# Turning a pair of heads' sums as they lie, and adding the two strips of keys on VectorE

## The reference

```python
qkv = _ln(x, ln1_g, ln1_b) @ w_in.T + b_in
q, k, v = ...                                  # 16 heads of 16
scores = einsum('bhqd,bhkd->bhqk', q, k) / sqrt(16)
allowed = (idx % 8 == 0)[:, None] | (idx[:, None] == idx[None, :])
attn = softmax(where(allowed, scores, -inf))
o = einsum('bhqk,bhkd->bhqd', attn, v)
x = x + o @ w_out.T + b_out
```

## Time and profile before

| | |
|---|---|
| median of 3 runs | 1451.54 us (1450.45 to 1452.65) |
| profiled execution, its own time | 1452.35 us |
| its span | 1450.6 us |
| PE busy | 1404.0 us, 97% |
| DVE busy | 846.5 us, 58% |
| ACT busy | 721.7 us, 50% |
| POOL busy | 649.0 us, 45% |
| mean granted TensorE clock | 0.993 of full speed |

### The profile page before, as it was taken

One profiled execution on the slowest core, in us unless ns is written; L12 is line 12 of the kernel. 1 busy time (PEld: TensorE's weight loads), 2 busy tenths in 40 slices (PEclk: granted clock), 3 DMA queues, 4 the chain that ended last, 5 costly groups with the idle time before them and its releaser, 6 DMA issues.

```text
span 1450.6 us, 26449 instructions
## 1 busy us (share of the span) xinstructions
PE 1404.0 (97%) x10167; PEld 1063.0 (73%) x10167; DVE 846.5 (58%) x1792; ACT 721.7 (50%) x1071; POOL 649.0 (45%) x533
## 2 busy tenths in 40 slices
PE   6889999999999999999999999999999999999997
PEld 4778655678888766668888866666888875557996
DVE  7747676636656666555647575763566556762332
ACT  3444555554444555554444555555344455555442
POOL 4554321338754414145865431333776441132755
PEclk9899999999999999999999999999999999999999
DMA  7464123215561222212682213220556212310100
GB/s 251 158 177 103 50 51 66 55 41 190 186 163 44 58 59 50 55 44 81 205 211 69 76 31 79 55 55 16 166 188 166 87 38 50 79 26 23 52 15 30
DMA packets 91393, 130.50 MB, mean 90 GB/s; under 512 B 8314, under 2 KB 68180, under 8 KB 88148
## 3 DMA queue, kind: packets, MB, share of 16 engines
q1 hardware_dynamic: 91268, 128.82, 32.2%
HBM read 68.08 MB, written 60.57 MB: 89 GB/s over the span
## 4 chain that ended last, share of the span: by engine, by line
PE 78%; DVE 11%; POOL 5%; issue 2%; ACT 1%; DMA 1%; SPq 0%; POOLq 0%; DVEq 0%; ACTq 0%
PE ps L1550 19%; PE ps L1551 16%; PE ps L1552 16%; PE ps L1739 9%; PE ps L1728 6%; PE ps L1713 4%; DVE mx L1428 3%; PE ps L1787 2%; DVE stats L1302 2%; PE ps L1775 2%; PE ps L1809 2%; POOL rows L1034 2%; PE ps L1745 1%; PE ps L1671 1%; DVE xn L1390 1%
## 5 line engine op out<-in xcount | busy, mean ns | idle before, releaser
L1428 DVE TENSOR_REDUCE mx<-ps 128x2 f32<-128x1024 f32 x256 | 311.1, 1223 | 189.9 <-PE ps L1713 188.3
L1157 ACT ACTIVATE prob<-ps 128x1024 f32<-128x1024 f32 x256 | 261.8, 1023 | 139.1 <-PE ps L1728 138.8
L1049 POOL TENSOR_TENSOR hid1l<-gel,hid1h 128x512 fp32r<-128x512 f32 x85 | 111.3, 1310 | 207.1 <-ACT hid1h L1199 206.9
L1049 POOL TENSOR_TENSOR hid2l<-gel,hid2h 128x512 fp32r<-128x512 f32 x85 | 111.4, 1311 | 201.6 <-ACT hid2h L1199 201.6
L1049 POOL TENSOR_TENSOR hid0l<-gel,hid0h 128x512 fp32r<-128x512 f32 x86 | 112.5, 1308 | 194.2 <-ACT hid0h L1199 194.2
L1191 ACT ACTIVATE gel<-ps,cols 128x512 f32<-128x512 f32 x128 | 88.1, 688 | 181.0 <-PE ps L1552 169.9
L1739 PE MATMUL ps<-prob,vals 128*32 128x256 f32 x2048 | 163.6, 391 | 0.0
L1193 ACT ACTIVATE gel<-ps 128x512 f32<-128x512 f32 x128 | 76.5, 598 | 170.6 <-PE ps L1809 170.6
L1728 PE MATMUL ps<-qslot,kslot 50*128 50x256 f32 x1024 | 128.9, 330 | 1.8 <-ACT prob L1157 1.8
L1728 PEld LDWEIGHTS ps<-qslot,kslot 50*128 50x128 f32 x1024 | 76.2, 184 | 66.5 <-issue 46.9
L1713 PE MATMUL ps<-kslot,qslot 48*128 48x512 f32 x512 | 102.3, 410 | 3.5 <-DVE mx L1428 3.0
(11 more groups left out here) (244 smaller groups left out, 3956.5 us busy)
## 6 DMA issues: line engine op xcount, KB each, us to landing
k_d<-kst SPq DMA_DIRECT2D x192, 128.0 KB
kslot<-k_d SPq DMA_DIRECT2D x64, 384.0 KB
xin<-in_L_attn_x SPq DMA_DIRECT2D x32, 256.0 KB, 4.0
rows<-xs_d SPq DMA_DIRECT2D x16, 512.0 KB, 6.0
y_d<-rows SPq DMA_DIRECT2D x15, 512.0 KB, 3.1
rows<-y_d SPq DMA_DIRECT2D x15, 512.0 KB, 4.3
out<-rows SPq DMA_DIRECT2D x15, 512.0 KB, 3.9
xs_d<-xin SPq DMA_DIRECT2D x28, 256.0 KB, 2.7
```

The lines of the kernel that those rows point to most:

```text
L1049: nc.gpsimd.tensor_tensor(hid[i % RING][1][:], gel[i % 2][:], hid[i % RING][0][:], ALU.subtract).then_inc(lo_done, 1)
L1157: nc.scalar.activation(prob[(n - 1) % 2][:].rearrange("p e i q -> p (e i q)"), ps[:, 0:2, :].rearrange("p a n -> p (a n)"), ACT.Exp).then_ ...
L1428: nc.vector.tensor_reduce(best[:, :, j % NQ], ps[:, at:at + 2, :], AX.X, ALU.max).then_inc(maxr_done, 1)
```

## The change

`fold` goes, with the instruction that makes it, and the three counts of the setup go down by one. PE turns each half of `oraw` with the plain identity: one transpose of 128 x 128 in the place of one product of 128 x 64. The result has 128 columns for a half in the place of 64, and the two strips lie beside one another. DVE copies the first strip of both halves to a new tile `osum` in SBUF (68 numbers for a partition), and adds the second strip from PSUM to it. It takes the reciprocal from `osum` and multiplies `osum` by it. The next user of the bank on PE waits for the addition (`osum_done`), and no longer for the multiplications (`otok_done`).

```diff
-COLS, BIN_DONE, CVB = 2, 9, 16
+COLS, BIN_DONE, CVB = 1, 8, 15
...
-                link(nc.vector.tensor_tensor(fold[:], ident[:, 0:2 * PR], ident[:, 2 * PR:4 * PR], ALU.add), False)
...
+        osum = keep("osum", [P, NQ, 2, VW])
...
-                    o = ps[:, BANK[(what, *a)], 0:NQ * 2 * PR].rearrange("p (t e v) -> p t e v", t=NQ, e=2)
-                    nc.vector.reciprocal(rsum[:], o[:, :, :, HD]).then_inc(rsum_done, 1)
+                    o = ps[:, BANK[(what, *a)], 0:NQ * P].rearrange("p (t i e v) -> p t i e v", t=NQ, i=2, e=2)
+
+                    nc.vector.tensor_copy(osum[:], o[:, :, 0, :, 0:VW]).then_inc(osum_done, 1)
+                    dve.wait_ge(osum_done, 2 * n - 1)
+                    nc.vector.tensor_tensor(osum[:], osum[:], o[:, :, 1, :, 0:VW], ALU.add).then_inc(osum_done, 1)
+                    dve.wait_ge(osum_done, 2 * n)
+                    nc.vector.reciprocal(rsum[:], osum[:, :, :, HD]).then_inc(rsum_done, 1)
                     dve.wait_ge(rsum_done, n)
                     for t in range(NQ):
                         nc.vector.tensor_tensor(
                             otok[:, t, PR * p:PR * (p + 1)].rearrange("p (e v) -> p e v", e=2),
-                            o[:, t, :, 0:HD], rsum[:, t, :, None].to_broadcast([P, 2, HD]), ALU.mult).then_inc(otok_done, 1)
+                            osum[:, t, :, 0:HD], rsum[:, t, :, None].to_broadcast([P, 2, HD]), ALU.mult).then_inc(otok_done, 1)
...
-                        pe.wait_ge(otok_done, NQ * N(what, *a))
+                        pe.wait_ge(osum_done, 2 * N(what, *a))
...
                     for t in range(NQ):
-                        last = mm(ps[:, bank, 2 * PR * t:2 * PR * (t + 1)], oraw[:, P * t:P * t + P], fold[:], start=t == 0, stop=True,
-                                  skip_group_check=True)
+                        last = nc.tensor.transpose(ps[:, bank, P * t:P * t + P], oraw[:, P * t:P * t + P], ident[:])
```

More of the change, by code:

```diff
@@ L627, in attention_ffn_kernel @@
         ident = keep("ident", [P, P])
-        fold = keep("fold", [P, 2 * PR])
         crow = keep("crow", [P, D])
@@ L757, in attention_ffn_kernel @@
         score_done, exp_done, av_done = sem("score_done"), sem("exp_done"), sem("av_done")
-        oraw_done, oturn_done, rsum_done, otok_done = (
-            sem("oraw_done"), sem("oturn_done"), sem("rsum_done"), sem("otok_done"))
+        oraw_done, oturn_done, osum_done, rsum_done, otok_done = (
+            sem("oraw_done"), sem("oturn_done"), sem("osum_done"), sem("rsum_done"), sem("otok_done"))
         ott_done, oth_done, otl_done, oproj_done, x1g_done = (
```

## The result

Over 22 runs of each the kernel before took 1449.35 us in the median and the changed kernel 1452.62 us. The ratio is 1.0018, 95% interval 1.0011 to 1.0026: 2.6 us slower (1.6 to 3.8). The forecast was no change, 0.6 us slower, 1452.1 us. The time lies in the forecast's range, the direction is the forecast's, and the size is four times what I gave. That the two times lie only 0.5 us apart is luck. I added my 0.6 to 1451.54 us, the median of three runs, which is 2.2 us above the median of the 22, and the change that I gave was 2.0 us too small.

A forecast was written before the change was run, and what follows sets the result against it. PE's own work was taken to bound the kernel, with waits on DVE. Batches 0 and 3 at +1.6 us each and 1 and 2 at -1.3 gave +0.6, from 1452.35 to 1452.95, less 0.81: 1452.1 us, range 1447.5 to 1456.5.

The forecast's parts named there:

- PE's saving: PE, each of 32 turns: two transposes take 0.20 to 0.22 us against 0.44 with `fold`; saves 0.22, 7.0 in all.
- Copy and addition: DVE at each turn: the copy of 68 numbers from PSUM takes 0.22 us, the addition 0.23.
- The hold: DVE multiplications, both operands now in SBUF: held until POOL's instruction ends; first ends 0.05 us behind it, second 0.10 later.
- The heavy turns: First and fifth turns of batches 0 and 3, `rows` addition behind: next `mx` product 1.07 us later, PE's saving lost.
- The third turn and the light ones: Batches 0, 3: third turn 0.20 us later; second, fourth, sixth 0.10, last two 0.22 earlier. Batches 1, 2: five, 0.22 earlier.
- other three: Three of the eight turns in batches 1 and 2: each gains between nothing and 0.2 us, some 0.2 together.
- later waits on DVE: Remaining case: later waits on DVE that a shifted order makes longer, slower, no size given; chance 0.08.
- A: The reciprocal on DVE, now reading SBUF alone, is held by POOL too: 4.0 us more, +4.6, 1456.1 us; chance 0.17.
- B: Nothing on DVE is held by POOL at the turns: -3.4 us, 1448.1 us; chance 0.15.
- C: DVE's delays are all covered and PE's full saving arrives: -7.0 us, 1444.5 us; chance 0.05.
- D: Two transposes take PE the same 0.44 us as the four short records, no saving: +4.7 us, 1456.2 us; chance 0.05.
- The signs that I named: Transposes 0.20 to 0.24 us; multiplications' longest over 1100 ns; reciprocal under 0.2 us; wrong if PE's reduction waits exceed 9.

The follow-up runs named there:

- e1: Changed kernel, but the sum is written back to PSUM, where reciprocal and multiplications read it; ratio 0.9970 against the kernel before, 1445.89 us.
- e2: Changed kernel with PE's part alone: copy and addition left out, DVE works on strip 0 only as before; ratio 0.9958 against the kernel before.
- e6: Changed kernel with POOL's low part of an item in two instructions of 256 columns instead of one of 512; ratio 1.0000 against the kernel before.

## Why the prediction was right, and where it was off

- **PE's saving.** Expected 0.22 us a turn, 7.0 in all; measured 0.27 at 20 turns and 0.19 to 0.23 at twelve, 7.9 in all. I took the pitch of four transposes (0.39 us for four) and halved it; two take 0.17. Where PE is the last, all of it arrives.
- **Copy and addition.** 0.22 and 0.23 us expected, 0.22 each measured.
- **The hold.** Right in mechanism, place and size: the pair ends 0.16 us behind POOL's instruction (0.15 expected), PE waits 1.17 us. e1 shows that it hangs on the operands: the pair stands at the same place of POOL's instruction, 0.49 us in, and is not held.
- **The heavy turns.** +1.07 expected, +1.19 measured. At the first product behind the first turn, where my sum ended, it is +1.05 (4.88 us behind the turn's start in the place of 3.83), and at a later product that waits for its reduction (190.27 in the changed kernel, 191.99 before) +1.16. The third turn and the light ones are within 0.05.
- **The failed step** is the sentence on the "other three" turns of an inner batch, "the same sum gives between nothing and 0.2". For the fifth turn the sum followed DVE to the first product behind it (-0.06) and stopped. The second stands behind 2 us of statistics, without slack. That is 0.77 us at each of two turns, 1.5 us. The heavy turns add 0.5, and the light turns, which gain more than I gave, take 0.8 back. Together this is 1.2 of the 2.0 us that the forecast was short of the measured time; the other 0.8 is not found in the distances, and lies within the interval of the measurement. The prediction had left 0.08 for "later waits on DVE", and a wait of that kind is what came.
- **The rivals.** A fell: the reciprocal from SBUF took 178 to 181 ns in all 32 instances, 17 of them wholly inside an instruction of POOL's. The Trainium skill, page "SBUF — State Buffer", section "SBUF: two separate sides", says of single operands that only those in a two-port mode are held, and the trace agrees for the reciprocal. B fell with the multiplications of 1307 ns; its case, nothing held, is what e1 built and measured: -4.4 us, -3.4 given. C fell with PE's waits of 1.17 us and the 2.6 us slower; e2, with DVE's part left out, shows that four kinds of turns give PE's saving away even so. D fell with the 0.17 us.
- **The signs that I named.** All came but two. The transposes take 0.17 us at most turns, and I had said 0.20 to 0.24. And I had called PE's waits for the reductions "over 9 us" a sign against me, and they are 9.8. My own terms (3.0 before, four waits of 1.3 at the heavy turns, 0.4 at each third) come to 9.0, so the bound was set too near. The fifth inner turns' 0.54 each went on top, and the sign pointed at the step that failed.

## What to carry to other kernels

Where a step moves its operands from PSUM to SBUF, look up which other instructions on VectorE with two SBUF operands were held by GpSimd in the same trace (longest against median of the line), and lay GpSimd's instruction beside the place: here the operands of a 0.19 us multiplication cost more than the two new instructions (4.4 us from e1 to the changed kernel in the sum of the distances, 3.2 from e2 to e1). The remedy is to keep one operand in PSUM, or to put the instruction behind the work that PE waits for. And follow a delay on a busy queue until the first gap in it, not only to the first instruction that somebody waits for: here the second one, behind 2 us of other work, had no slack.

## What the runs showed of the hardware

- A VectorE multiplication with both operands in SBUF that falls due inside a GpSimd subtraction ends 0.05 us behind it, and a second one that follows 0.10 to 0.15 later; with one operand in PSUM it takes its 0.19 us (changed kernel and e1).
- Where a second GpSimd subtraction follows at once (e6), the first of two such multiplications ends 0.05 us behind the first subtraction in all 18 cases, and the second one is held to the end of the second subtraction in 17 of the 18.
- Splitting GpSimd's 128 x 512 subtraction into two of 128 x 256 costs it 1.43 us in the place of 1.30, and made the kernel before, otherwise unchanged, 0.28% faster (0.15 to 0.40).
- From the first weight load to the next group two transposes of 128 x 128 take 0.17 us at 20 turns, against 0.44 for the four records of the product with `fold`; four transposes took 0.39.
